# A cross-attention and FP4 feed-forward kernel: quantization by halves, shorter GpSimd instructions, another prologue, a third score bank, and one VectorE instruction for four maxima banks

## The reference

```
x = x + attention(layernorm(x), ctx, ctx)      # softmax(q k^T / 4) v, then Wo, bo
n = layernorm(x)
gate = fp4(n) @ fp4(w_gate).T ;  up = fp4(n) @ fp4(w_up).T
h = silu(gate) * up
x = x + fp4(h) @ fp4(w_down).T
fp4(y): scale = max(|block of 16|) / 6 ; round(y / scale) to the grid 0, .5, 1, 1.5, 2, 3, 4, 6 ; times scale
```

## Time and profile before

| what | value |
|---|---|
| median of 3 runs | 1791.18 us (1790.6 to 1791.48) |
| the profiled execution | 1790.86 us, of which 1789.1 us are its span |
| PE busy | 1658.9 us, 93% |
| VectorE busy | 1432.7 us, 80% |
| ScalarE busy | 1133.2 us, 63% |
| GpSimd busy | 526.3 us, 29% |
| mean TensorE clock granted | 0.978 of full |

### The profile page before, as it was taken

The page is one execution under the profiler, slowest core; times in us unless marked ns, Lnnn a source line. Parts: engine busy times, 40 slices in busy tenths (PEclk is TensorE's granted clock), DMA queues, the critical chain, the costliest instruction groups (busy, mean ns, idle before and its releaser), DMA issues.

```text
span 1789.1 us, 26605 instructions
## 1 busy us (share of the span) xinstructions
PE 1658.9 (93%) x9408; PEld 655.9 (37%) x9408; DVE 1432.7 (80%) x2032; ACT 1133.2 (63%) x2293; POOL 526.3 (29%) x409
## 2 busy tenths in 40 slices
PE   4798889999999999999999999999999999989968
PEld 2332224333433334333443334333443333313325
DVE  6777888878778887879888787788878797788538
ACT  2367567766667667676667666676676766666631
POOL 4316340442107220253204421072202531012203
PEclk8899899999999999999999999999999999999989
DMA  5644432142324313352331423244132422200000
GB/s 147 147 71 110 97 83 44 47 111 57 61 43 108 86 34 55 60 128 48 64 56 51 109 55 61 43 109 89 32 60 54 91 46 53 54 7 10 13 21 12
DMA packets 106224, 117.50 MB, mean 66 GB/s; under 512 B 22884, under 2 KB 87404, under 8 KB 106092
## 3 DMA queue, kind: packets, MB, share of 16 engines
q1 hardware_dynamic: 101408, 111.54, 29.5%
q10 hardware_dynamic: 4684, 4.27, 1.0%
HBM read 76.78 MB, written 30.16 MB: 60 GB/s over the span
## 4 chain that ended last, share of the span: by engine, by line
PE 77%; DVE 12%; ACT 5%; issue 3%; DMA 1%; ACTq 0%; POOL 0%; SPq 0%; DVEq 0%; POOLq 0%
PE pvb L780 20%; PE st L751 20%; PE mx L765 10%; PE misc L687 7%; DVE cmx L1012 5%; PE misc L645 5%; PE misc L652 5%; ACT prob L937 4%; PE misc L699 2%; PE misc L707 2%; PE misc L666 2%; PE misc L695 1%; PE misc L631 1%; PE misc L728 1%; DVE ht L1041 1%
## 5 line engine op out<-in xcount | busy, mean ns | idle before, releaser
L937 ACT ACTIVATE prob<-st 128x512 f32<-128x512 f32 x1630 | 886.5, 598 | 425.2 <-PE st L751 422.6
L1012 DVE TENSOR_REDUCE cmx<-mx 128x2 f32<-128x1024 f32 x768 | 906.1, 1220 | 194.7 <-PE mx L765 191.6
L751 PE MATMUL st<-qstack,kstack 112*128 112x512 bf16 x1630 | 514.1, 387 | 36.2 <-ACT prob L937 23.5
L780 PE MATMUL pvb<-prob,vv 128*32 128x512 f32 (+1 forms) x3328 | 446.7, 609 | 0.6 <-ACT prob L937 0.6
L751 PEld LDWEIGHTS st<-qstack,kstack 112*128 112x128 bf16 x1630 | 130.2, 99 | 527.6 <-issue 255.0
L765 PE MATMUL mx<-kstack,qstack 48*128 48x512 bf16 (+1 forms) x2048 | 254.7, 339 | 26.9 <-DMA qstack<-scr_q 15.8
L1315 POOL TENSOR_TENSOR ht<-ht,rh 128x704 f32<-128x704 f32 x29 | 40.3, 1388 | 420.5 <-DVE rh L988 420.5
L687 PE MATMUL misc<-wguT,rowsT 128*128 128x352 f32 x456 | 153.7, 458 | 0.0
L1279 POOL TENSOR_TENSOR cin<-cin 128x400 f32<-128x400 f32 (+1 forms) x60 | 55.3, 922 | 278.7 <-ACT cin L872 278.7
L765 PEld LDWEIGHTS mx<-kstack,qstack 48*128 48x128 bf16 x2048 | 57.9, 94 | 198.2 <-issue 154.5
L780 PEld LDWEIGHTS pvb<-prob,vv 128*32 128x32 f32 (+1 forms) x3328 | 66.0, 109 | 138.8 <-issue 124.0
(11 more groups left out here) (196 smaller groups left out, 1564.4 us busy)
## 6 DMA issues: line engine op xcount, KB each, us to landing
kstack<-scr_k SPq DMA_DIRECT2D x384, 100.1 KB, 4.4
scr_k<-cin SPq DMA_DIRECT2D x48, 300.0 KB, 3.4
qstack<-scr_q SPq DMA_DIRECT2D x372, 32.0 KB, 1.9
cin<-ctx_in SPq DMA_DIRECT2D x8, 1280.0 KB, 6.6
scr_q<-qp SPq DMA_DIRECT2D x15, 384.0 KB, 5.4
scr_k<-cin SPq DMA_DIRECT2D x16, 300.8 KB, 5.3
xn<-x SPq DMA_DIRECT2D x8, 512.0 KB, 3.9
att<-pvs SPq DMA_DIRECT2D x128, 32.0 KB, 1.9
```

Source lines behind the costliest of these rows:

```text
L751: mm(score_bank(it, n, pair, h)[0:KROWS[kt], :], kstack[:, hd, KOFF[kt]:KOFF[kt] + KROWS[kt]], qstack[:, hd, :], start=True, stop=True).th ...
L780: last = mm(pvb[2 * D * h:2 * D * (h + 1), :], vv[0:w, kt, (HG * g + h) // 2, D * (h % 2):D * (h % 2 + 2)], prob[0:w, n % 2, h, :], start= ...
L937: activate(prob[0:KROWS[kt], n % 2, 2 * pair + h, :], score_bank(it, n, pair, h)[0:KROWS[kt], :], ACT.Exp, scale=SCALE).then_inc(exp_done[ ...
L1012: v.tensor_reduce(cmx[:, g % 2, h0:h0 + 2, at:at + 1], products, op=ALU.max, axis=AX.X).then_inc(max_free, 1)
```

## The change

The diff, cut to its core:

```diff
-    6: ([("o", 1, "late")], []),
-    7: ([("xnT", 0, "early")], []),
+    6: ([("xnT", 0, "early")], []),
+    7: ([("o", 1, "late")], []),
...
-    5: ([("ctx2", j, "early") for j in range(7)], []),
-    8: ([("xnT", j, "early") for j in range(2)], []),
+    5: ([("ctx2", j, "early") for j in range(3)] + [("xnT", j, "early") for j in range(2)] + [("ctx2", 3, "early")], []),
+    9: ([("q", 0, "early")], []),
+    10: ([("ctx2", j, "early") for j in range(4, 7)], []),
     11: ([("k", j, "early") for j in range(4)], []),
-    14: ([("q", 0, "early")], []),
     34: ([("q", 1, "early")], []),
...
-    7: [("late", "mean", 0)], 8: [("late", "root", 0)], 9: [("late", "apply", 0)], 10: [("att", "nm", 1)], 11: [("late", "apply", 1)], 12: [("late", "xmax", 0)],
-    13: [("late", "xscale", 0)], 14: [("late", "xmul", 0)], 15: [("late", "xpower", 0)], 17: [("late", "xlast", 0)],
+    2: [("late", "values", 4)], 3: [("late", "values", 5)], 4: [("late", "values", 6)], 5: [("late", "values", 7), ("late", "stats", 0)],
+    7: [("late", "stats", 1), ("late", "mean", 0)], 8: [("late", "root", 0)], 9: [("late", "apply", 0)], 10: [("att", "nm", 1)],
+    11: [("late", "xscale", 0)], 12: [("late", "xpower", 0)], 13: [("late", "apply", 1)], 14: [("late", "xscale", 1)], 15: [("late", "xpower", 1)],
+    16: [("late", "xlast", 0)], 17: [("late", "xlast", 1)],
...
-    0: [("late", "bias", 0)], 10: [("early", "k", 0)], 11: [("early", "k", 1)], 12: [("early", "q", 0)], 13: [("early", "k", 2)],
-    14: [("early", "k", 3)], 15: [("early", "k", 4)], 16: [("late", "xround", 0)], 17: [("early", "k", 5), ("early", "q", 1)], 18: [("early", "k", 6)], 19: [("early", "k", 7)],
+    0: [("late", "bias", 0)], 10: [("early", "k", 0)], 11: [("early", "k", 1)], 12: [("early", "q", 0)], 13: [("late", "xround", 0), ("early", "k", 2)],
+    14: [("early", "k", 3)], 15: [("early", "k", 4)], 16: [("late", "xround", 1), ("early", "q", 1)], 17: [("early", "k", 5)], 18: [("early", "k", 6)], 19: [("early", "k", 7)],
     24: [("late", "hscaled", 0)], 25: [("late", "hround", 0)], 28: [("late", "hscaled", 1)], 29: [("late", "hround", 1)],
...
+                banks = [0, 1] + [2] * (kind != "loop" and not any(step)) + [3, 4] * (kind == "last" and n >= WIDE)
+                for h in range(HG):
+                    b = min(banks, key=lambda c: turn.get(c, -3))
...
+        def rows_rounding(it, k):
+            return mt[:, 0:512] if it.kind == "tail" else ht[:, :, :].rearrange("p t n -> p (t n)")[:, 512 * k:512 * (k + 1)]
...
+        def piece_rounding(p):
+
+            _, rows, n = raw_piece(p)
+            return mt[0:rows, 0:n] if p % 2 == 0 else rowsT[:, :, :].rearrange("p c n -> p (c n)")[0:rows, 0:n]
...
                 sp.wait_ge(c_link, 4)
+                queries_out(it, 0)
                 keys_out(it, 0, range(4))
...
+                def maxima_of_two(one, two):
+
+                    part, q, g, _, h0, piece = one
+                    dve.wait_ge(max_full, it.count(part, M_BATCH, q + 2))
+                    at, to = (p // FULL * (FULL + 1) + p % FULL for p in (piece, two[5]))
+                    v.tensor_reduce(cmx[:, g % 2, h0:h0 + 2, at:to + 1:to - at], mx[:, :, :, :].rearrange("p b h n -> p h b n"), op=ALU.max, axis=AX.X).then_inc(max_free, 2)
...
-                    elif what == "xmax":
-                        link(v.tensor_reduce(ax[:, :], blocks(xa[:, :]), op=ALU.max, axis=AX.X, apply_absolute_value=True), part)
                     elif what == "xscale":
-                        link(scaled(sx[:, :], ax[:, :]), part)
-                        link(v.reciprocal(rx[:, :], sx[:, :]), part)
-                        link(below(rx[:, :]), part)
-                    elif what == "xmul":
-                        link(v.tensor_tensor(blocks(xa[:, :]), blocks(xa[:, :]), over(rx[:, :]), ALU.mult), part)
+                        cols = slice(32 * k, 32 * (k + 1))
+                        link(v.tensor_reduce(ax[:, cols], blocks(halves[k]), op=ALU.max, axis=AX.X, apply_absolute_value=True), part)
+                        link(scaled(sx[:, cols], ax[:, cols]), part)
+                        link(v.reciprocal(rx[:, cols], sx[:, cols]), part)
+                        link(below(rx[:, cols]), part)
                     elif what == "xpower":
-                        if "early" in it.parts:
-                            dve.wait_ge(full["q"], it.count("early", 2, 2))
-                        link(v.tensor_scalar(mt[:, :].bitcast(I32), xa[:, :].bitcast(I32), EXPONENT, None, ALU.bitwise_and), part)
-                        v.tensor_scalar(mt[:, :], mt[:, :], 1.0, ROUND, ALU.max, ALU.mult).then_inc(xm_ready, 1)
+                        y, m = halves[k], rows_rounding(it, k)
+                        link(v.tensor_tensor(blocks(y), blocks(y), over(rx[:, 32 * k:32 * (k + 1)]), ALU.mult), part)
+                        link(v.tensor_scalar(m.bitcast(I32), y.bitcast(I32), EXPONENT, None, ALU.bitwise_and), part)
+                        last = v.tensor_scalar(m, m, 1.0, ROUND, ALU.max, ALU.mult)
+                        if it.kind != "tail":
+                            last.then_inc(xm_ready, 1)
+                        else:
+                            link(last, part)
+                            link(v.tensor_tensor(y, y, m, ALU.add), part)
+                            link(v.tensor_tensor(y, y, m, ALU.subtract), part)
...
-                        dve.wait_ge(xr_ready, c(1, 1))
-                        v.tensor_tensor(blocks(xa[:, :]), blocks(xa[:, :]), over(sx[:, :]), ALU.mult).then_inc(xq_ready, 1)
+                        if it.kind != "tail":
+                            dve.wait_ge(xr_ready, c(2, k + 1))
+                        y = halves[k]
+                        v.tensor_tensor(blocks(y), blocks(y), over(sx[:, 32 * k:32 * (k + 1)]), ALU.mult).then_inc(xq_ready, 1)
...
                 def weight_powers(p):
-                    w, rows, n = raw_piece(p)
-                    m = mt[0:rows, 0:n]
+                    w, m = raw_piece(p)[0], piece_rounding(p)
                     dve.wait_ge(wy_ready, p + 1)
-                    if p:
-                        dve.wait_ge(wq_done, p)
-                    else:
+                    if p >= 2:
+                        dve.wait_ge(wq_done, p - 1)
+                    elif p == 0:
                         dve.wait_ge(full["q"], it.count("early", 2, 2))
...
-                    for job in todo:
-                        maximum(job)
+                    while todo:
+                        one = todo.pop(0)
+                        if todo and one[1] % 2 == 0 and todo[0][4] == one[4] and todo[0][5] < M_HEADS - 1:
+                            maxima_of_two(one, todo.pop(0))
+                        else:
+                            maximum(one)
...
-                g_.memset(kstack[32:64, heads, :].bitcast(F32), 1.0 + 2.0 ** -23 * 0x3F80).then_inc(c_link, 1)
-                g_.memset(qstack[32:64, heads, :].bitcast(F32), 0.0).then_inc(c_link, 1)
+                for hd in range(heads.start, heads.stop):
+                    last = g_.memset(kstack[32:64, hd, :].bitcast(F32), 1.0 + 2.0 ** -23 * 0x3F80)
+                last.then_inc(c_link, 1)
+                for hd in range(heads.start, heads.stop, 2):
+                    last = g_.memset(qstack[32:64, hd:hd + 2, :].bitcast(F32), 0.0)
+                last.then_inc(c_link, 1)
...
+            def short(out, in0, in1, op):
+
+                n = out.shape[1] // 256
+                w = out.shape[1] // n
+                for j in range(n):
+                    cols = slice(j * w, (j + 1) * w)
+                    last = g_.tensor_tensor(out[:, cols], in0[:, cols], in1[:, cols], op)
+                return last
...
+            def short_scaled(y, sc):
+                n = y.shape[1] // 256
+                w = y.shape[1] // n // NB
+                for j in range(n):
+                    part = blocks(y)[:, j * w:(j + 1) * w, :]
+                    last = g_.tensor_tensor(part, part, over(sc[:, j * w:(j + 1) * w]), ALU.mult)
+                return last
...
                     elif what == "xround":
-                        m = mt[:, :]
-                        pool.wait_ge(xm_ready, c(1, 1))
-                        g_.tensor_tensor(xa[:, :], xa[:, :], m, ALU.add).then_inc(xr_step, 1)
-                        pool.wait_ge(xr_step, c(1, 1))
-                        g_.tensor_tensor(xa[:, :], xa[:, :], m, ALU.subtract).then_inc(xr_ready, 1)
+                        y, m = halves[k], rows_rounding(it, k)
+                        pool.wait_ge(xm_ready, c(2, k + 1))
+                        short(y, y, m, ALU.add).then_inc(xr_step, 1)
+                        pool.wait_ge(xr_step, c(2, k + 1))
+                        short(y, y, m, ALU.subtract).then_inc(xr_ready, 1)
...
                     if it.kind == "pre" and n == 15:
+
+                        pool.wait_ge(k_split[0], 4)
                         pool.wait_ge(q_split, 1)
```

165 lines of the change are left out of this document (75 added, 90 removed).

## The result

The changed kernel takes 1821.59 us (median of four runs, 1820.27 to 1822.96) against 1790.93 of the kernel before beside it: 1.0171 times as long, with an interval of 1.0153 to 1.0189. The forecast was slower, 1797.4; the time lies above the range's upper end of 1813. The profiled execution has a span of 1820.6, 31.5 more than before.

What follows compares the result with a forecast made beforehand. PE was taken to bound the loop, with little to win. Terms 7.7 + 5.4 - 5 - 5 - 20.5 - 6 + 18 + 7.2 + 10.7 - 3 - 3 = +6.5 on 1790.86 gave 1797.4 us, range 1776 to 1813.

Steps and rivals of the forecast that it cites:

- What bounds the kernel: Whole kernel: PE bounds the loop, busy 194.35 of 200 us; cheaper VectorE or GpSimd instructions pay only where PE waits.
- The clock: Loop, behind the new gaps at k4 and k7: PE's clock falls 6.3 times at 1.7 us, +10.7 (0 to 20).
- k4 and k7: Loop, GpSimd roundings ahead of k2, q1 and k5 delay ACT: k4 +18 (15 to 22.5), k7 +7.2 (5 to 9).
- The prologue and the catch-up: Fused maxima hold up closely following products: prologue +7.7 (6 to 12.5), ten catch-up steps of `first` +5.4 (3 to 7).
- Weights in `first`: Steps 20 to 23 and 30 to 33: short GpSimd instructions, second rounding buffer, third score bank win -5 (0 to -9).
- the move of "values 3": Loop, nm 3 and values 3 later: h's transposes no longer wait for VectorE, -6 (0 to -7.3).
- The tail: Tail: fewer VectorE excesses beside GpSimd, against a later first half from shared statistics, -3 (-6 to +2).
- six such excesses of about 1 us are in reach: Tail: VectorE operations lengthened beside GpSimd, such as 2.12 us instead of 1.05 on 704 columns, could be shortened.
- The delay of the first half: Tail: statistics shared by both halves let the first half start about 2 us later.
- the clock stays up: Rival: no clock fall behind the new gaps, as in iteration 1, giving 1786.7 us; chance 0.21.
- rounding first costs nothing: Rival: "xpower" 0 done before q0 ends, or k2's buffer not needed by then, giving 1761.5 us; chance 0.10.
- the fused reduction holds up ordinary steps: Rival: in loop steps extras exceed the 0.57 us slack, 0.3 in 8 of 52 steps, +17, 1814; chance 0.14.

Runs made afterwards that it cites:

- e1_k2: Changed kernel with one edit: on GpSimd the rounding of the first half stands behind k2 instead of ahead of it; 1794.7 us, 1.0026 of before.
- e1_single: Changed kernel with its order kept but one reduction for each maxima product, as before the change; 1805.02 us, 1.0087 of before.
- e1_fused: Kernel before with the fused reduction alone; 1811.39 us, 1.012 of before.
- e2_moves: Kernel before with only the job moves: o1 and xnT 0 exchanged, second half's statistics behind it, nm 3 and values 3 later; 1762.07 us, 0.9844 of before.
- e3_long: The fastest kernel with long GpSimd instructions again (512, 704 or 1024 columns in one); 1753.82 us, 0.9788 of before.
- experiment 4: Changed kernel with k2 and k5 moved ahead, single reductions in prologue and catch-up, plus the tail's norm and quantization half by half; 1748.36 us, 0.9764 of before.

## Why the prediction was off

- **What bounds the kernel** held. Only changes at places where PE waits moved the time, and the fused reduction, 347 times 0.07 us of VectorE, gave nothing where it was hidden.
- **The clock** is one of the two terms that failed. "By the same share it falls behind k4's 3 us in 4.3 of six, and behind the shorter one of k7 in perhaps 2" took seven old gaps of 2 us as a frequency for gaps that are longer, 3.4 and 3.0. All twelve were followed by the low level, and so were the six of k7 in e1_k2 and the twelve in e1_single, of 2.8 us or more (0.68 or lower in the 4.4 us behind each): thirty of thirty. What stands behind the idle time costs 12.0 us at k4 and 6.8 at k7, 8.2 more than the 10.7 of the sum. A single fall is not always 1.7: it was 1.8 behind k4 and 1.1 behind k7, where PE is busy for only 3.8 of the 4.6 us. I had taken k7's gap by what the change added (1.2) and not by its whole length (3.0 us). The window that the prediction reads for iteration 1, 312.0 to 316.6, holds the gap itself; the 4.6 us behind it (from 314.5) are at 1.00 too, so that reading stands.
- **k4 and k7** were the right mechanism, and their length is the other term that failed. PE idles 3.41 us at k4 (3.69 in iteration 1) where 3.0 was worked out, and 2.0 more than before at k7 (2.3 in iteration 1) where 1.2 was: 33.0 us in all instead of 25.2, 7.8 more. With the clock's 8.2 this is the 16.0 that the two lines of the table miss. Both chains priced instructions at their undisturbed length, and VectorE's queue as empty when the products of step 12 were done. But VectorE and GpSimd lengthen each other: an extra of step 11 took 0.94 instead of 0.26, which is more than the 0.54 that the reduction came late, and GpSimd's passes took 1.61 and 1.40 instead of 1.16 and 0.94. The trace of before had such passes in every loop iteration, 1.81 and 1.75 us of k's last pass beside VectorE's operations on 1024 columns; the prediction took the 0.95 of another:

```profile
767.22 1.81 POOL L1283 TENSOR_TENSOR cin<-cin 128x401 bf16<-128x401 f32 x1
...
779.70 1.75 POOL L1283 TENSOR_TENSOR cin<-cin 128x400 bf16<-128x400 f32 x1
```

- **The prologue and the catch-up**: 3.07 a step instead of 3.02, and some steps at the lower clock, which was in the bounds but not in the value: +2.9. The rule from the Trainium skill, Perfetto Trace Analysis, section Optimizing Tensor Performance (independent groups should rotate through PSUM banks, so that taking one out overlaps the next group's matmuls) agrees with the trace there, and only there: the period rose from 2.31 to 3.07, while in the loop taking the rotation away cost 0.24 us per iteration.
- **Weights in `first`**: half of the 9 us was taken, and 2.3 came. By step, the weights' two stretches (20 to 23 and 31 to 33) gave 3.2 us in after, and six steps without a job gave 2.6 (step 25 takes 3.07 instead of 3.48; without the third bank it is 3.49 again). Steps 39 and 40 lost 3.0, and this has no term in the sum: the move of "values 3" was priced for the loop, but in `first` it brings them to step 38, behind the scales of the weights' fifth piece (L1233). The two of them hold VectorE for 3.5 us ahead of a reduction, and the products of step 40 wait 2.49 us for it:

```profile
250.08 0.88 DVE L1233 TENSOR_REDUCE ah<-ht 128x44 f32<-128x704 f32 x1
...
251.82 0.94 DVE L1120 RECIPROCAL sums<-sums 128x128 f32<-128x128 f32 x1
...
252.79 0.86 DVE L1122 TENSOR_TENSOR att<-att,sums 128x128 f32<-128x128 f32 x1
...
253.58 2.28 DVE L1049 TENSOR_REDUCE cmx<-mx 128x4 f32<-128x2048 f32 x1
...
255.91 0.83 PE L809 MATMUL mx<-kstack,qstack 48*128 48x65 bf16 x10 [2.49 <-DVE cmx L1049]
```

  Steps 39 and 40 take 7.01 us in before and in e1_fused, which have "values 3" at step 36, and 9.30 to 10.28 in all eleven kernels that have it at 38, e2_moves with single reductions and nothing else among them. So it is the move, and the fused reduction adds little. With long instructions in the fastest kernel 5.8 us of `first` go again, with two score banks 6.2; each of the two is worth about what was given to all of them together. The Trainium skill, SBUF — State Buffer, section SBUF: two separate sides, has the port pair that VectorE and GpSimd share as a lock held for a whole instruction; the 2.46 us beside 2.35 in e3_long agree with it.
- **The tail**: -3 was forecast, +1.6 came, within its range. The step that failed is that "six such excesses of about 1 us are in reach". They are hardly on the path: in the tail of before PE waits 8.62 us for the first half's norm, and behind it only 1.41 and 0.71 us for VectorE. The delay of the first half, named as about 2, is what counted (10.48 instead of 8.62), and experiment 4 gives it back.
- **The rivals**: that the clock stays up is contradicted by the twelve gaps. That rounding first costs nothing is contradicted by k4's 3.93 us of idle time. That the fused reduction holds up ordinary steps holds for one step, at 0.24 us an iteration instead of 2.4.

The fastest kernel of this study, 1748 to 1749 us, is the changed one with k2 ahead of the first rounding, k5 ahead of q1, single reductions in the prologue and the catch-up, and the tail half by half: 2.4% under the kernel before.
